# Sending each pair's spectra a second time with real and imaginary halves exchanged, so that a cross product is one full-width instruction

## The chip, the cores and the metric

The kernel runs on one core of one Trainium2 chip. The metric is the device time of one execution in microseconds; the median of three runs is given. The engines are TensorE (PE; PEld is its weight load), VectorE (DVE), ScalarE (ACT), GpSimd (POOL) and SyncE (SP, which only issues DMAs here).

## The reference, cut to what matters

The program is one block of a network: a convolution part with a filter in the frequency domain, then a mixture of experts. The change lies in the filter:

```python
xp = jnp.einsum('bhwc,mc->bhwm', xc, w_pw1)
xp = star_scale * jnp.square(jax.nn.relu(xp)) + star_bias
xf = jnp.fft.rfft2(xp, axes=(1, 2), norm='ortho')
weight = jnp.einsum('bfc,hwf->bhwc', routeing.astype(cw.dtype), cw)
spatial_weight = jnp.einsum('bfc,hwf->bhwc', spatial_routeing, spatial_weights)
xs = jnp.fft.irfft2(xf * weight, s=(H, W), axes=(1, 2), norm='ortho')
out = xp * spatial_weight + xs
out = jnp.einsum('bhwm,dm->bhwd', out, w_pw2)
...
x = x + conv(ln_c(x))
t = to_tokens(x)
t = t + ffn(ln_t(t), gate_w, w1, w3, w2)      # top 2 of 8 experts
```

The batch is 16 images of 16 x 16 pixels with 128 channels (256 inside the filter). `xf * weight` is a complex product.

## The kernel before

**Stages.** The images are handled in eight pairs. Phase A (to about 100 us) computes, for each pair, the star activation, its forward transform by matmul (`forward`, copied to `spec` by `spectrum_copy`) and the two routing networks. Then the routing weights are computed and written into the table `RS` by eight DMAs of 64 KB, four partitions each (`routing_rows`: five on SP's queue, three on GpSimd's). Phase B (131 to 224 us) is the filter, with the changed code. Behind it come the routing of tokens to experts, the expert loop over 71 tiles and the weighted sum of the results.

**The spectra.** A transform of 256 pixels is split by the parity of the vertical frequency into two parts, e = 0 and 1, of 128 rows each. In `spec[:, e, pair, :]` partition n holds a real component and partition n + 64 the imaginary component of the same frequency; the 512 columns are two images times 256 channels.

**The complex product** takes two products and a sum. TensorE writes the filter's weights for a pair into three PSUM banks in turn (`filters`, six matmuls a pair, waited for by `b_w`). VectorE's `filter_products(i, e)` forms `prod` (spectrum times real weights, L1069) and `cross` (spectrum of the *other* 64 partitions times imaginary weights). Since the two halves have to be exchanged, and a VectorE instruction has all its partitions in one order, `cross` is made by two instructions of 64 partitions, L1072 and L1073. GpSimd adds the two (`spectral`, L490), TensorE transforms back (`branch`, L817 and L823) and projects (`project`, L833).

**Order in phase B.** Every engine runs through its own fixed list; semaphores tie them together. VectorE's list for step i (`phase_b`) is: `filter_products(i + 1, 0)`, `residual(i - 1)` with the statistics of the tokens (L1078, L954, L958), `filter_products(i + 1, 1)`, `normalise_tokens(i - 1)` (L964, four instructions), `logit_copy(i - 2)` (L1090). GpSimd's is: `spatial(i + 1)` (two products, L484), `inv_std(i - 1)` (L427, L429), `spectral(i + 1)` (two sums, L490). SP's list there is only `store_tn`: for each pair one DMA of 256 KB that writes the normalised tokens `xn` to `tn_dram`, after waiting for `b_norm`. Steps 0 to 2 and 7 are written out, 3 to 6 are a hardware loop of two steps a turn. SP's list is cut differently: steps 0, 1, 6 and 7 are written out.

**Names.** `b_cross` counts finished cross products, two a pair; `a_spec` counts finished spectrum copies; `b_norm` normalised pairs; `r_mm` is set when the matmuls that read `rw2` (a table of the routing network) are done.

Of the kernel before, what the change touches and what calls it, by code (L numbers as in the profile page):

```python
# [18 lines left out]
ALU = mybir.AluOpType  # L19
# [7 lines left out]
ds = bass.ds  # L27

P = 128
# [147 lines left out]
def metaformer(nc, io):  # L177
    with ExitStack() as ctx:
# [65 lines left out]
        shared = sb("shared", [P, 7680])  # L244
        rw2 = sb("rw2", [P, NF * MED])
        idx_g = [sb(f"idx_g{u}", [P, 4], U32) for u in range(2)]
        idx_s = [sb(f"idx_s{u}", [P, 4], U32) for u in range(2)]
# [17 lines left out]
        def area(tensor, first_col):  # L265
# [63 lines left out]
            "r_log r_max r_sub r_exp r_sum r_rec r_norm r_tr r_hi r_lo r_rows r_rows_pool b_w b_sw b_p b_cross b_u b_y "  # L329
            "b_vt b_vts b_w2 b_t b_stats b_aggr b_eps b_rstd b_norm b_tn0 b_tn1 b_tr b_tnt "  # L330
            "b_gate b_logit q_iota q_zero q_tri q_dve q_ready q_exp_done q_count q_oh_tile q_oh_ready q_oh_used "
# [28 lines left out]
        def _(sp):  # L360
# [30 lines left out]
            routing_rows(sp, range(5), "r_rows")  # L391

            def store_tn(i, u):
                sp.wait_ge(S["b_norm"], i + 1)
                sp.dma_start(tn_dram[ds(i * (4 * P), 4 * P), :].rearrange("(p q) d -> p q d", p=P),
                             xn[:, u, :, :]).then_inc(S[f"b_tn{u}"], 16)
            pair_loop(sp, store_tn)

# [552 lines left out]
        def _(dve):  # L951
# [111 lines left out]

            def filter_products(i, e):

# [5 lines left out]
                dve.wait_ge(S["b_w"], i * 6 + n_s + 1)  # L1071
                dve.tensor_tensor(cross[e][0:64], spec_at(64, P, e, i), ps_w[n_s % 3][0:64, :], ALU.mult)  # L1072
                dve.tensor_tensor(cross[e][64:P], spec_at(0, 64, e, i), ps_w[n_s % 3][64:P, :], ALU.mult)\  # L1073
                    .then_inc(S["b_cross"], 1)
# [52 lines left out]
            def phase_b(i, u):  # L1127
                if not last(i, PAIRS):
                    filter_products(i + 1, 0)
                if not first(i):  # L1130
                    residual(i - 1, 1 - u)
                if not last(i, PAIRS):
                    filter_products(i + 1, 1)
                else:

                    dve.wait_ge(S["q_iota"], 8 + BUFS)
                    dve.wait_ge(S["b_logit"], PAIRS - 3)
                    top_two(0, EARLY)
                if not first(i):
                    normalise_tokens(i - 1, 1 - u)  # L1140
                if not isinstance(i, int) or 2 <= i < PAIRS - 1:
                    logit_copy(i - 2, u)
            filter_products(0, 0)
            filter_products(0, 1)
            spectrum_copy(PAIRS - 1)
# [189 lines left out]
```

## Time and profile before

| | |
|---|---|
| median of 3 runs | 529.23 us (526.0 to 530.99) |
| span of the profiled execution, first to last instruction | 477.8 us |
| median less that span | 51.4 us |
| mean granted TensorE clock over the span | 0.893 |
| filter phase, one pair (VectorE, 183.18 to 194.20 us) | 11.02 us |
| of it busy: TensorE, VectorE, GpSimd, ScalarE | 9.62, 10.63, 6.21, 2.90 us |
| VectorE busy over the span | 272.9 us, 57% |

### The profile page before, as it was taken

The page shows a single profiled execution, that of the slowest core. Times are in us where ns is not written, and L with a number is a line of the kernel's source. Part 1 is how long each engine was busy: PE and PEld are TensorE (multiplying, and loading weights), DVE is VectorE, ACT ScalarE, POOL GpSimd, SP SyncE. Part 2 cuts the span into 40 slices and gives each one's busy share as a digit, 9 for nine tenths or more (in the row PEclk, how much of TensorE's full clock was granted, in tenths as well). Part 3 has the DMA queues.
Part 4 walks back from the last instruction along what each step waited for, and adds up shares of the span by engine and source line. Part 5 has one row for each costly group of instructions (what it writes and reads, how often), then busy time and mean ns, then how long its engine had stood idle before and what let it go on. Part 6 is the DMA issues. An engine that isn't in the chain of part 4 may idle for free.

```text
span 477.8 us, 8130 instructions
## 1 busy us (share of the span) xinstructions
PE 359.2 (75%) x2236; PEld 292.9 (61%) x2237; DVE 272.9 (57%) x673; ACT 162.8 (34%) x374; POOL 260.3 (54%) x267
## 2 busy tenths in 40 slices
PE   0899999895199988875007699999999999998500
PEld 0555555393058777764006599887987888887400
DVE  5367675614077999996898554444434444433245
ACT  0454543302013223211400355443444444443253
POOL 7333342512176655541650667777777777777444
PEclk9999999978579999999555599999999999998955
DMA  8920000000200000004600111111111111112194
GB/s 249 248 63 1 2 0 0 1 5 9 35 1 1 23 22 32 34 24 152 287 0 1 45 40 54 50 52 49 54 51 49 55 50 49 52 54 50 42 358 162
DMA packets 14081, 29.94 MB, mean 63 GB/s; under 512 B 4392, under 2 KB 5564, under 8 KB 13548
## 3 DMA queue, kind: packets, MB, share of 16 engines
q1 hardware_dynamic: 7388, 17.93, 12.1%
q0 software_dynamic: 4784, 9.52, 6.7%
q10 hardware_dynamic: 1888, 2.23, 1.3%
q8 instruction: 11, 0.18, 0.2%
q14 instruction: 10, 0.08, 0.1%
HBM read 20.24 MB, written 8.85 MB: 61 GB/s over the span
## 4 chain that ended last, share of the span: by engine, by line
PE 35%; DVE 26%; DMA 13%; issue 12%; POOL 8%; ACT 2%; DVEq 1%; POOLq 1%; SPq 1%; ACTq 0%
PE bank L927 8%; DVE xn L964 7%; DMA y_dram<-shared,idx_s 7%; PE bank L909 6%; PE bank L902 3%; DMA RS<-r_hl 3%; PE bank L772 2%; PE bank L715 2%; PE bank L723 2%; POOL shared L490 2%; DVE st L954 2%; DMA shared<-tn_dram,idx_g 2%; PE bank L734 2%; DVE spec L1179 2%; PE bank L888 2%
## 5 line engine op out<-in xcount | busy, mean ns | idle before, releaser
L518 POOL DMA_INDIRECT shared<-tn_dram,idx_g x71 | 68.8, 968 | 39.9 <-DVE idx_g L1217 18.6
L527 POOL DMA_INDIRECT y_dram<-shared,idx_s x71 | 70.0, 986 | 27.1 <-issue 12.8
L909 PE MATMUL bank<-spec,shared 128*128 x426 | 61.2, 280 | 1.8 <-DVE shared L1233 0.7
L1247 DVE TENSOR_TENSOR shared<-shared,bank 128x384 f32<-128x384 f32 x71 | 39.3, 554 | 36.4 <-ACT shared L672 35.4
L672 ACT ACTIVATE shared<-bank 128x384 f32<-128x384 f32 x71 | 34.8, 490 | 64.3 <-PE bank L927 64.3
L909 PEld LDWEIGHTS bank<-spec,shared 128*128 128x128 f32 x426 | 53.5, 193 | 5.1 <-issue 5.0
L927 PE MATMUL bank<-RS,xgt_hl 128*128 x142 | 55.5, 391 | 0.6
L964 DVE TENSOR_SCALAR xn<-T,mv,rstd 128x128 f32<-128x128 f32 (+1 forms) x64 | 51.4, 874 | 5.1 <-POOL rstd L429 4.6
L927 PE MATMUL bank<-w_hi,xgt_hl 128*128 x142 | 48.9, 345 | 0.0
L427 POOL TENSOR_SCALAR var_eps<-mv 128x4 f32<-128x4 f32 x16 | 3.7, 229 | 68.7 <-DVE mv L958 68.6
L1228 DVE TENSOR_TENSOR xgt_hl<-bank,xgt_hl 128x128 fp32r<-128x128 f32 x71 | 20.6, 290 | 33.7 <-ACT xgt_hl L660 33.7
L902 PE MATMUL bank<-ident,shared 128*128 128x128 f32 x213 | 36.0, 278 | 4.5 <-DVE shared L1247 4.5
L660 ACT ACTIVATE xgt_hl<-bank 128x128 fp32r<-128x128 f32 x71 | 19.7, 277 | 57.8 <-PE bank L896 57.8
L799 PE MATMUL bank<-RS,coef 128*128 128x512 f32 (+1 forms) x48 | 21.4, 503 | 22.3 <-DMA RS<-r_hl 15.7
L927 PE MATMUL bank<-w_lo,xgt_hl 128*128 x142 | 37.3, 345 | 0.0
L665 ACT ACTIVATE shared<-bank 128x384 f32<-128x384 f32 x71 | 34.5, 486 | 5.9 <-PE bank L902 5.8
L734 PE MATMUL bank<-xp,sp 128*64 128x256 f32 x288 | 33.8, 388 | 0.0
L902 PEld LDWEIGHTS bank<-ident,shared 128*128 128x128 f32 x213 | 27.0, 142 | 10.8 <-DVE shared L1247 8.7
L823 PE MATMUL bank<-inv,shared 128*128 128x256 f32 x128 | 30.4, 380 | 1.8 <-POOL shared L490 1.8
L927 PEld LDWEIGHTS bank<-RS,xgt_hl 128*128 128x128 f32 x142 | 27.5, 194 | 5.7 <-issue 5.2
L734 PEld LDWEIGHTS bank<-xp,sp 128*64 128x64 f32 x288 | 20.2, 139 | 13.3 <-issue 4.2
L927 PEld LDWEIGHTS bank<-w_hi,xgt_hl 128*128 128x128 f32 x142 | 27.7, 195 | 0.0
(171 smaller groups left out, 680.0 us busy)
## 6 DMA issues: line engine op xcount, KB each, us to landing
star<-y_dram SPq DMA_DIRECT2D x16, 256.0 KB, 5.4
star<-in_w SPq DMA_DIRECT2D x2, 1536.0 KB, 8.5
tn_dram<-xn SPq DMA_DIRECT2D x8, 256.0 KB, 2.0
out<-T ACTq DMA_DIRECT2D x8, 256.0 KB, 2.3
spec<-in_w SPq DMA_DIRECT2D x1, 1536.0 KB, 13.2
shared<-in_sp_even SPq DMA_DIRECT2D x1, 1280.0 KB, 13.2
shared<-tn_dram,idx_g POOLq DMA_INDIRECT x71, 2.5
y_dram<-shared,idx_s POOLq DMA_INDIRECT x71, 2.2
```

Source lines behind the costliest of these rows:

```text
L518: pool.indirect_dma_start(xg[b], None, tn_dram, bass.IndirectOffsetOnAxis(ap=idx_g[quad][:, col:col + 1], axis=0)).then_inc(S[f"g_x{b}"], 16)
L527: pool.indirect_dma_start(y_dram, bass.IndirectOffsetOnAxis(ap=idx_s[quad][:, col:col + 1], axis=0), yo[b], None).then_inc(S[f"y_out{b}"], 16)
L665: act.activation(hidt[u], p_ht[u][:, 0:HID], ACT.Copy).then_inc(S["f_hts"], 1)
L672: act.activation(silu[u], p_h1[u][:, 0:HID], ACT.Silu).then_inc(S["f_silu"], 1)
L734: mm = pe.matmul(ps_conv[u][HALF * g:HALF * g + HALF, 0:PIX], sp1[:, t, :], xp[:, u, g, t // 3:t // 3 + SIZE, t % 3:t % 3 + SIZE], start=( ...
L799: pe.matmul(ps_w[n % 3][:, :], coef[:, ring[n], :], RS[:, :, :, ds(i, 1), :].rearrange("r c g b m -> r g c (b m)"), start=True, stop=True)\
L823: mm = pe.matmul(ps_v[u][m][:, g * PIX:(g + 1) * PIX], y_c[u][e][:, g * MED + m * P:g * MED + (m + 1) * P], inv[:, e, :], start=False, sto ...
L902: mm = pe.transpose(p_ht[u][:, c * P:(c + 1) * P], hid[u][:, c * P:(c + 1) * P], ident[:, :])
L909: mm = pe.matmul(p_y[:, 0:DIM], hidt[u][:, c * P:(c + 1) * P], w2s[:, c, ds(e * DIM, DIM)], start=(c == 0), stop=(c == HC - 1))
L927: mm = pe.matmul(psum[:, 0:HID], xgt[u][xs], w_hl[ws][:, cols], start=(n == 0), stop=(n == 2))
L964: op = dve.tensor_scalar(xn[:, u, t, :], flat(T[:, ds(i * 4 + t, 1), :]), mv[:, u, t, 0:1], rstd[:, u, t:t + 1], ALU.subtract, ALU.mult)
L1247: dve.tensor_tensor(hid[u], silu[u], p_h3[u][:, 0:HID], ALU.mult).then_inc(S["f_act"], 1)
```

## The change

SP sends each pair's spectra once more, from `spec` into one of two buffers of 128 partitions x 1024 columns, with partitions 0 to 63 and 64 to 127 exchanged. That is two DMAs a pair, of 64 partitions x 2 parts x 2 KB, 256 KB each. The buffers are used in turn: `rw2`, free once the routing matmuls are done, for even pairs, and the new `turned_b` for odd ones. Pairs 0 and 1 are sent behind SP's routing rows. Pair i + 2 is sent in SP's step i, ahead of that step's store of normalised tokens, after waiting for the spectrum copy and for the cross products of pair i. VectorE's cross product of both halves is then one instruction, which waits for the pair's two DMAs (`b_turned0`, `b_turned1`, 32 counts a pair).

```diff
+        turned_b = sb("turned_b", [P, NF * MED])
+        turned = [t[:].rearrange("p (e n) -> p e n", e=2) for t in (rw2, turned_b)]
...
+            def turn_spectrum(i, u):
+                wait_apart(sp, S["a_spec"], i * 2 + 2)
+                wait_done(sp, S["b_cross"], i * 2 - 2)
+                for lo, hi in ((0, 64), (64, 0)):
+                    sp.dma_start(turned[u][lo:lo + 64], spec[hi:hi + 64, :, ds(i, 1), :].rearrange("p e i n -> p e (i n)"))\
+                        .then_inc(S[f"b_turned{u}"], 16)
+
             def store_tn(i, u):
                 sp.wait_ge(S["b_norm"], i + 1)
                 sp.dma_start(tn_dram[ds(i * (4 * P), 4 * P), :].rearrange("(p q) d -> p q d", p=P),
                              xn[:, u, :, :]).then_inc(S[f"b_tn{u}"], 16)
-            pair_loop(sp, store_tn)
+            sp.wait_ge(S["r_mm"], 1)
+            turn_spectrum(0, 0)
+            turn_spectrum(1, 1)
+
+            def turn_and_store(i, u):
+                if not deferred(i):
+                    turn_spectrum(i + 2, u)
+                store_tn(i, u)
+            pair_loop(sp, turn_and_store)
...
-            def filter_products(i, e):
+            def filter_products(i, u, e):
...
                 dve.wait_ge(S["b_w"], i * 6 + n_s + 1)
-                dve.tensor_tensor(cross[e][0:64], spec_at(64, P, e, i), ps_w[n_s % 3][0:64, :], ALU.mult)
-                dve.tensor_tensor(cross[e][64:P], spec_at(0, 64, e, i), ps_w[n_s % 3][64:P, :], ALU.mult)\
+                dve.wait_ge(S[f"b_turned{u}"], (i - u) * 16 + 32)
+                dve.tensor_tensor(cross[e], turned[u][:, e, :], ps_w[n_s % 3][:, :], ALU.mult)\
                     .then_inc(S["b_cross"], 1)
```

`deferred(i)` is true for steps 6 and 7, which have no pair i + 2. The calls of `filter_products` pass the buffer's number.

SP's list before, from the routing rows into the loop (the two `tn_dram` DMAs ahead of the loop are the stores of pairs 0 and 1):

```order
L352 DMA RS<-r_hl 4x32x128 [waits rs_zero,r_lo,r_hi]
L352 DMA RS<-r_hl 4x32x128 x4
L395 DMA tn_dram<-xn 128x512 [waits b_norm] x2
L132 UNCONDITIONAL_BRANCH
L132 ISA
L395 ISA [waits b_norm]
L395 DMA tn_dram<-xn 128x512
```

and in the changed kernel at the same place:

```order
L401 DMA rw2<-spec 64x2x512 [waits a_spec,r_mm]
L401 DMA rw2<-spec 64x2x512
L401 DMA turned_b<-spec 64x2x512 [waits a_spec]
L401 DMA turned_b<-spec 64x2x512
L401 DMA rw2<-spec 64x2x512 [waits b_cross,a_spec]
L401 DMA rw2<-spec 64x2x512
L406 DMA tn_dram<-xn 128x512 [waits b_norm]
L401 DMA turned_b<-spec 64x2x512 [waits b_cross,a_spec]
L401 DMA turned_b<-spec 64x2x512
L406 DMA tn_dram<-xn 128x512 [waits b_norm]
```

The transfers of pair 3, the last ones here into `turned_b`, stand behind the store of pair 0; in the same way those of pairs 4 to 7 stand behind the stores of pairs 1 to 4.

VectorE's list before, in step 1 (products of pair 2, residual of pair 0):

```order
L1069 TENSOR_TENSOR shared<-spec,bank 128x512 [waits b_y,b_w]
L1072 TENSOR_TENSOR shared<-spec,bank 64x512 [waits b_w]
L1073 TENSOR_TENSOR shared<-spec,bank 64x512
L1078 TENSOR_TENSOR T<-T,bank 128x512 [waits b_w2]
L954 BN_STATS st<-T 128x6 [waits b_t]
```

and in the changed kernel at the same place:

```order
L1088 TENSOR_TENSOR shared<-spec,bank 128x512 [waits b_y,b_w]
L1092 TENSOR_TENSOR shared<-rw,bank 128x512 [waits b_turned0,b_w]
L1097 TENSOR_TENSOR T<-T,bank 128x512 [waits b_w2]
L973 BN_STATS st<-T 128x6 [waits b_t]
```

One instruction stands where two stood, with one more wait ahead of it. (`rw` in a name is `rw2`; `shared` holds `prod` and `cross`, `bank` is PSUM.)

## Rows read from the trace of the kernel before

**Rows 1.** The page's first part: busy time, share of the span, instructions.

```profile
PE 359.2 (75%) x2236; PEld 292.9 (61%) x2237; DVE 272.9 (57%) x673; ACT 162.8 (34%) x374; POOL 260.3 (54%) x267
```

**Rows 2.** VectorE's timeline, one pair: start, duration, engine, line, operation, idle before.

```profile
178.92 0.68 DVE L1069 TENSOR_TENSOR shared<-spec,bank 128x512 f32<-128x512 f32 x1
179.62 0.68 DVE L1072 TENSOR_TENSOR shared<-spec,bank 64x512 f32<-64x512 f32 x1
180.32 0.69 DVE L1073 TENSOR_TENSOR shared<-spec,bank 64x512 f32<-64x512 f32 x1
...
185.32 4.48 DVE L964 TENSOR_SCALAR xn<-T,mv,rstd 128x128 f32 x4
...
189.94 0.68 DVE L1069 TENSOR_TENSOR shared<-spec,bank 128x512 f32<-128x512 f32 x1
```

**Rows 3.** Busy time by stretch (the columns are named in the first line).

```profile
core 0: us, PE busy (x) PEld busy (x) DVE busy (x) ACT busy (x) POOL busy (x), PEclk, DMA share, GB/s
183.18:194.20 11.02, 9.62 (x60) 8.16 (x58) 10.63 (x21) 2.90 (x5) 6.21 (x6) 1.00 0.06 24
94.00:96.00 2.00, 0.00 (x0) 0.00 (x0) 1.94 (x4) 0.84 (x2) 2.00 (x4) 0.86 0.00 0
8.00:14.00 6.00, 1.09 (x4) 0.72 (x4) 3.84 (x9) 1.22 (x1) 5.45 (x5) 1.00 1.14 397
14.00:22.00 8.00, 7.19 (x32) 4.68 (x34) 2.17 (x4) 3.38 (x7) 1.09 (x1) 1.00 1.01 209
...
179.80:180.60 0.80, 0.80 (x6) 0.78 (x7) 0.79 (x2) 0.59 (x2) 0.00 (x0) 1.00 0.84 328
...
118.00:130.00 12.00, 0.00 (x0) 0.00 (x0) 0.00 (x0) 0.00 (x0) 3.08 (x3) 0.50 0.34 39
```

**Rows 4.** Timeline: GpSimd's last product and the last normalise instruction of a pair; a later normalise.

```profile
177.42 1.27 POOL L484 TENSOR_TENSOR shared<-star,shared 128x512 f32<-128x512 f32 x1
...
177.47 1.31 DVE L964 TENSOR_SCALAR xn<-T,mv,rstd 128x128 f32 x1
...
215.82 1.12 DVE L964 TENSOR_SCALAR xn<-T,mv,rstd 128x128 f32<-128x128 f32 x4
```

**Rows 5.** GpSimd's timeline for the pair of rows 2.

```profile
183.35 0.23 POOL L427 TENSOR_SCALAR var_eps<-mv 128x4 f32<-128x4 f32 x1 [4.65 <-DVE mv L958]
183.73 1.04 POOL L429 TENSOR_TENSOR rstd<-var_eps,mhalf 128x4 f32<-128x4 f32 x1 [0.15 <-POOL var_eps L427]
184.74 2.50 POOL L490 TENSOR_TENSOR shared<-shared 128x512 f32<-128x512 f32 x2
187.19 2.53 POOL L484 TENSOR_TENSOR shared<-star,shared 128x512 f32<-128x512 f32 x2
```

**Rows 6.** The chain that ended last, start of the filter phase: start, us, what.

```profile
115.63 0.61 SPq L352
...
118.07 12.03 DMA RS<-r_hl
...
132.57 0.68 DVE shared L1072
...
147.91 0.69 DVE shared L1073
148.63 0.70 DVE T L1078
```

**Rows 7.** TensorE's timeline: the forward transform of pair 7.

```profile
133.18 3.48 PE L723 MATMUL bank<-buf,fwd 128*128 128x512 f32 x4
```

**Rows 8.** SP's timeline: issue of a load to 64 partitions; issue of a store of tokens.

```profile
9.56 0.59 SPq L377 DMA_DIRECT2D shared<-in_sp_even  x1
...
178.96 0.35 SPq L395 DMA_DIRECT2D tn_dram<-xn  x1
```

**Rows 9.** DMA issues by line: KB each, median us from issue to landing.

```profile
tn_dram<-xn SPq DMA_DIRECT2D x8, 256.0 KB, 2.0
```

More of the change, by code:

```diff
@@ L329, in metaformer @@
             "r_log r_max r_sub r_exp r_sum r_rec r_norm r_tr r_hi r_lo r_rows r_rows_pool b_w b_sw b_p b_cross b_u b_y "
-            "b_vt b_vts b_w2 b_t b_stats b_aggr b_eps b_rstd b_norm b_tn0 b_tn1 b_tr b_tnt "
+            "b_vt b_vts b_w2 b_t b_stats b_aggr b_eps b_rstd b_norm b_turned0 b_turned1 b_tn0 b_tn1 b_tr b_tnt "
             "b_gate b_logit q_iota q_zero q_tri q_dve q_ready q_exp_done q_count q_oh_tile q_oh_ready q_oh_used "
@@ L1128, in phase_b @@
                 if not last(i, PAIRS):
-                    filter_products(i + 1, 0)
+                    filter_products(i + 1, 1 - u, 0)
                 if not first(i):
@@ L1132, in phase_b @@
                 if not last(i, PAIRS):
-                    filter_products(i + 1, 1)
+                    filter_products(i + 1, 1 - u, 1)
                 else:
@@ L1142, in phase_b @@
                     logit_copy(i - 2, u)
-            filter_products(0, 0)
-            filter_products(0, 1)
+            filter_products(0, 0, 0)
+            filter_products(0, 0, 1)
             spectrum_copy(PAIRS - 1)
```

## Prediction

> **What bounds the kernel now.** I started at the page's totals [rows 1]: no engine is full over the span, so shares say nothing and the stage of the change has to be read by itself. That stage is the filter phase, from about 131 to 224 us. VectorE's timeline for one pair [rows 2] shows no gaps: the reader should lay the starts end to end and find the first product of the next pair 11.02 us after this one (178.92 to 189.94). The table by stretch [rows 3] has the same 11.02 us with 10.63 us of VectorE, 9.62 of TensorE and 6.21 of GpSimd. TensorE has 1.4 us of slack and its clock is at its upper level of 2.4 GHz (granted 1.00).
>
> VectorE is not bound by its own work alone. The normalise takes 4.48 us in this stretch [rows 2] and 1.12 us when GpSimd is quiet [rows 4]. GpSimd's timeline [rows 5] says why: once the aggregate is done it computes var_eps and rstd, then two sums (L490) and two products (L484), 184.74 to 189.72. Each of the four normalise instructions ends just behind one of these four: the last product starts at 177.42 and ends at 178.69, the last normalise starts at 177.47 and ends at 178.78 [rows 4]. So the loop that sets the 11.02 us is: cross product of spectrum part 0, residual, statistics, aggregate (VectorE), then rstd and four full-width operations (GpSimd), whose end frees the last normalise, then the product and again the cross product. The cross product of part 1 runs beside GpSimd's rstd and is not in the loop.
>
> **What is removed.** Sixteen products lose one of their two half instructions. The second half starts 0.70 us after the first [rows 2], and the full-width product of the same 512 columns takes 0.68 us, as much as one half; so each saves 0.70 us of VectorE, 11.2 in all. What of it lies on the path:
> - Part 0 of pairs 2 to 7 is in the loop (for pair 2 the chain runs through L1073 at 147.91 straight into the residual at 148.63 [rows 6]): 6 x 0.70 = 4.2 us.
> - Part 1 of these pairs: nothing. The normalise would begin at 184.8 instead of 185.32, since rstd ends at 184.77 [rows 5], but GpSimd's first sum has started at 184.74 and the last of the four still ends at 189.72.
> - Pair 0: nothing. Behind its products come the copies of pair 7's spectrum, and these need the forward transform that TensorE has in work from 133.18 to 136.66 [rows 7]. Pair 1: its products lie beside TensorE, for which VectorE waits again before pair 2.
>
> How the normalise gives way decides the term for part 1. The trace: 1.12 us becomes 4.48, in four steps that end with GpSimd's four instructions. The Trainium skill (SBUF — State Buffer, "Who interferes with whom") says that VectorE and GpSimd share a port pair under "an exclusive lock" and that the loser waits out the whole instruction. By that rule an earlier start buys nothing, as I have it; if the two only shared bandwidth, a start 0.5 us earlier would give some 0.5 us more per pair, 3 us in all. The rows side with the rule.
>
> **What is added.** Per pair two transfers of 256 KB from SBUF to SBUF, 64 partitions each, on SP's queue, and a wait of the cross product on both. What matters is where SP issues them. For pairs 3 to 7 they stand directly behind a store of normalised tokens: SP takes up the transfers of pair i+3 only after it has issued the store of pair i, and that waits for the normalise of pair i. In VectorE's order this normalise is the last long piece before the products of pair i+3: in the trace its end (178.78) lies 0.84 us before the cross product (179.62). So whatever the transfers need beyond 0.84 us stops VectorE, five times, and queued behind the stopped cross product are the residual, the statistics, the aggregate, and through it GpSimd's rstd and the next normalise. The buffer's release (the cross products of pair i+1 done) came long before and isn't what SP waits for.
>
> Time from the end of the normalise: the store is issued 0.18 us later (178.96) and keeps SP for 0.35 [rows 8], so to 0.53; with 0.1 for registers (my estimate, from the 0.18 before) the first transfer is issued at 0.65. A transfer over 64 partitions keeps SP for 0.59 (the table load at 9.56 [rows 8]), so the second is issued at 1.25. The store's bytes move from 179.8 to 180.6, 0.84 after its issue [rows 3], and it has landed 2.0 us after its issue [rows 9]: 0.36 for the last leg. So the engines are busy with the store from 1.02 to 1.82, and the first transfer's bytes could start at 1.49 but follow at 1.82. The rate: loads over 128 partitions moved 397 GB/s, and then, when the tables of 64 partitions were in flight, 209 [rows 3]. These transfers are of the second kind: 262,144 bytes / 209 GB/s = 1.25 us each. End of bytes 1.82 + 2 x 1.25 = 4.32, landed 4.68. The stop is 4.68 - 0.84 = 3.84 us.
> - Lower end: both move at 397 GB/s, 0.66 each: landed at 3.50, stop 2.66.
> - Upper end: reading and writing 64 partitions each cost 1.25 and don't overlap: landed at 7.2, stop 6.3. The only SBUF to SBUF rows of size, the routing rows, do worse (five of 64 KB in 14.5 us, from the issue at 115.63 to 130.10, where the landing lets TensorE go [rows 6]), but each goes to 4 partitions; I leave them as a warning, not as a rate.
> I take 3.84, from the row of the same shape. Five stops: 19.2 us (13.3 to 31.7).
>
> The Trainium skill (SBUF — State Buffer, "The DMA setup-cost knee") gives a transfer 2 us plus its bytes at 436 GB/s. For the 256 KB store that is 2.6 us, where the row has 2.0. For both new transfers as one of 512 KB, issued at 0.65, it would be 3.2 us, landed at 3.85, a stop of 3.0 and five of them 15.0: 4.2 us less than my term. The row's own duration is used.
>
> **The start of the phase.** SP issues the transfers of pairs 0 and 1, 1 MB, right behind the routing rows, whose landing TensorE awaits (12.03 us of the chain [rows 6]). Queued later they can't go first, but they load the same engines and partitions. Bounds: 0, and 5.0 us (1 MB at 209 GB/s) if the routing rows had to wait for all of it. I take 1.0, near the low end, since they move only 39 GB/s from 118 to 130 [rows 3]. Pair 0's own transfers cost nothing: its cross product came at 132.57 [rows 6], 2.5 us after the routing rows; without that cover it would be up to 2.5 more. Pair 2's are issued once pair 0's products are done, near 136, and have until 147. One wait I cost at nothing: the store of normalised tokens now shares its queue, but its buffer is needed two pairs, 22 us, later.
>
> **TensorE's clock.** A stop of VectorE leaves TensorE idle, about 1.4 + 3.1 us in a pair. From 94 to 96 us it did nothing, and the granted clock fell from 1.00 to 0.50 (mean 0.86 [rows 3]), its level of 1.2 GHz. It may fall here too, but a pair then has 14.2 us for 9.62 us of matmuls, so a few microseconds at half speed fit in. I take 0, at most 2 in the tail behind pair 7.
>
> **Sum.** 19.2 - 4.2 + 1.0 = +16.0 us. The span of the profiled execution is 477.8 us; the median of the runs shown is 529.2, 51.4 more, which lies around the span and isn't touched. 529.2 + 16.0 = 545.2 us, 3.0% slower.
>
> **Rivals.**
> - *The transfers overlap or run at full rate* (stop 2.66): 13.3 - 4.2 + 1.0 = +10.1, 539.3 us. For it: one goes to the upper and one to the lower 64 partitions. Against: tables for both halves were in flight together from 14 to 22 us and moved 209 GB/s.
> - *Reading and writing in series* (stop 6.3): +28.5, 557.7 us. Against it: no row shows a transfer that pays twice.
> - *The transfers are hidden and only the saving counts.* The place is VectorE's cross product of part 0; the price is nothing and the gain 4.2, less 1.0 at the start: 526.0 us, a little faster, not measurably. It decides once the transfers land within 0.84 us of the normalise's end; at a stop of 0.6 us per pair the two sides balance. Against it: the shortest landing of 256 KB is 2.0 us, and SP has to issue the store first.
> - *TensorE becomes the bound*: if the clock stays at 1.2 GHz the 9.62 us become 19.2 against 14.2, five times 5.1 more: 570.6 us. Against it: after each stop comes dense work.
>
> **How the numbers follow.** Forecast 0.55, full rate 0.22, in series 0.10, hidden 0.06, clock 0.05, and 0.02 for something slower that I don't see. Range 536 to 556: it takes in the full rate with no cost at the start, and a stop near 5.5; outside are the hidden case, the clock and most of the series case. A measurement can tell about 1% (5.3 us) from no change. Faster by more 0.02, within 0.06, slower 0.92.
>
> **What would show it.** In the changed trace: cross products of 0.69 us, 16 in all; an idle of 3 to 4 us ahead of that of part 0 for pairs 3 to 7 alone, released by the transfer, and none for pairs 0 to 2; a pair's period near 14.2; the normalise still at 4.4; the two transfers issued within 1.3 us of the store. It is wrong if SP reaches the transfers before the store (no idle), if the idle ends with TensorE, or if the routing rows land several microseconds later.

## The result and the profile after

The changed kernel takes 553.88 us (median of 4 runs, 553.36 to 554.66); the kernel before, timed beside it, 529.45 us (4 runs, 526.0 to 530.99). The ratio is 1.0475, with a 95% interval of 1.0435 to 1.0515: 24.4 us slower, where 16.0 were forecast. Ratios leave out executions that lie over 1.5% above the fastest of their kernel; the traced execution of one experiment, the one without transfers, is of that kind, so only lengths inside its filter phase are read from it.

The page of the changed kernel, first part, against [rows 1]: VectorE has 16 instructions and 9.8 us less to do, and the kernel is slower all the same.

```profile
PE 378.2 (68%) x2236; PEld 313.3 (57%) x2237; DVE 263.1 (48%) x657; ACT 161.5 (29%) x374; POOL 260.9 (47%) x267
```

VectorE's timeline, changed kernel, from pair 3's cross product of part 0 to pair 4's (start, duration, line, operation, in brackets the idle time before and what ended it):

```profile
165.36 0.69 DVE L1092 TENSOR_TENSOR shared<-turned_b,bank 128x512 f32<-128x512 f32 x1 [5.21 <-DMA turned_b<-spec]
165.97 0.68 DVE L1097 TENSOR_TENSOR T<-T,bank 128x512 f32<-128x512 f32 x1
...
169.45 4.98 DVE L983 TENSOR_SCALAR xn<-T,mv,rstd 128x128 f32<-128x128 f32 x4 [0.30 <-POOL rstd L448]
174.35 0.18 DVE L1109 COPY logits<-bank 128x32 f32<-128x32 f32 x1
174.45 0.67 DVE L1088 TENSOR_TENSOR shared<-spec,bank 128x512 f32<-128x512 f32 x1
179.62 0.69 DVE L1092 TENSOR_TENSOR shared<-rw,bank 128x512 f32<-128x512 f32 x1 [4.50 <-DMA rw<-spec]
180.23 0.68 DVE L1097 TENSOR_TENSOR T<-T,bank 128x512 f32 x1
```

Against [rows 2] the reader should see two things. The cross product is one instruction of 0.69 us (L1092), and the residual (L1097) starts 0.61 us behind it. And the cross product of part 0 waits for the transfer: 5.21, 4.50, 4.63, 4.86 and 5.01 us for pairs 3 to 7, together 24.2, and not at all for pairs 0 to 2. The residuals of the next pairs follow at 194.90, 209.81 and 224.86, so a pair takes 14.3 to 15.1 us instead of 10.7 to 11.0.

SP's timeline of the changed kernel: L356 are the routing rows, L401 the new transfers, L406 the store of normalised tokens.

```profile
115.34 2.98 SPq L356 DMA_DIRECT2D RS<-r_hl  x5
118.42 1.83 SPq L401 DMA_DIRECT2D rw<-spec  x2
120.29 4.16 SPq L401 DMA_DIRECT2D turned_b<-spec  x2
138.03 1.27 SPq L401 DMA_DIRECT2D rw<-spec  x2
159.58 0.35 SPq L406 DMA_DIRECT2D tn_dram<-xn  x1
160.04 1.28 SPq L401 DMA_DIRECT2D turned_b<-spec  x2
174.45 0.34 SPq L406 DMA_DIRECT2D tn_dram<-xn  x1
175.32 1.36 SPq L401 DMA_DIRECT2D rw<-spec  x2
```

From 159.58 on each pair of transfers stands directly behind a store that waits for the normalise, as the prediction read from the order. Pair 4 by its own terms: the normalise ends at 174.43, the first transfer is issued at 175.32. The table by stretch shows its bytes (last column GB/s; the first row is the store's):

```profile
175.30:176.00 0.70, 0.70 (x5) 0.57 (x4) 0.00 (x0) 0.00 (x0) 0.00 (x0) 1.00 0.92 363
176.40:176.80 0.40, 0.40 (x5) 0.33 (x4) 0.00 (x0) 0.40 (x2) 0.00 (x0) 1.00 0.55 133
176.80:177.20 0.40, 0.40 (x5) 0.40 (x4) 0.00 (x0) 0.40 (x1) 0.00 (x0) 1.00 0.87 189
177.20:177.60 0.40, 0.40 (x4) 0.35 (x3) 0.00 (x0) 0.04 (x1) 0.00 (x0) 1.00 1.03 200
177.60:178.00 0.40, 0.40 (x4) 0.35 (x3) 0.00 (x0) 0.00 (x0) 0.00 (x0) 1.00 0.87 195
178.00:178.40 0.40, 0.40 (x4) 0.35 (x3) 0.00 (x0) 0.00 (x0) 0.00 (x0) 1.00 1.03 369
178.40:178.80 0.40, 0.40 (x4) 0.35 (x3) 0.00 (x0) 0.00 (x0) 0.00 (x0) 1.00 0.70 225
178.80:179.20 0.40, 0.40 (x5) 0.40 (x4) 0.00 (x0) 0.23 (x1) 0.00 (x0) 1.00 0.00 0
176.60:178.70 2.10, 2.10 (x13) 1.92 (x12) 0.00 (x0) 0.64 (x2) 0.00 (x0) 1.00 0.95 248
```

The last row takes nearly all the bytes of the pair together: they flow from 176.6 to 178.7, at 189 to 200 GB/s up to about 178.0 and faster, up to 369, in the last 0.7 us. On average that is 248 GB/s, somewhat more than the 209 of [rows 3]. The cross product starts at 179.62, 0.9 us behind the last of them.

At the start of the phase, the chain that ended last and TensorE's timeline, against the 12.03 us of [rows 6]:

```profile
117.78 15.92 DMA RS<-r_hl
```

```profile
133.79 3.19 PE L818 MATMUL bank<-RS,coef 128*128 128x512 f32 x6 [19.55 <-DMA RS<-r_hl]
...
231.09 3.48 PE L842 MATMUL bank<-inv,shared 128*128 128x256 f32 x8 [2.94 <-POOL shared L509]
```

The routing rows land 3.6 us later than before (TensorE started at 130.19 there). While they are under way, the DMA engines are busy for 0.96 of the time, where [rows 3] had 0.34 (changed kernel):

```profile
118.00:130.00 12.00, 0.00 (x0) 0.00 (x0) 0.00 (x0) 0.00 (x0) 2.81 (x3) 0.53 0.96 98
```

The last row of TensorE's timeline is eight inverse transforms behind pair 7, for the most part at half the clock; before, the same eight took 1.99 us:

```profile
209.31 1.99 PE L823 MATMUL bank<-inv,shared 128*128 128x256 f32 x8 [1.78 <-POOL shared L490]
```

The granted clock over the phase was 0.86, where before it was 1.00 (changed kernel first, then the kernel before; each row from the residual of pair 0 to that of pair 5):

```profile
151.00:224.86 73.86, 59.95 (x312) 51.55 (x310) 46.98 (x91) 15.48 (x27) 31.20 (x31) 0.86 0.19 54
```

```profile
148.63:203.10 54.47, 48.87 (x295) 41.49 (x294) 52.79 (x100) 14.87 (x26) 31.04 (x30) 1.00 0.06 24
```

**The sum by the trace.** Start +3.60; stops +24.2; products faster -6.0 (1.17 up to pair 0's residual, then 0.96 to 0.98 in each of the five intervals between residuals, stop taken off, as the one with pair 4's stop: 14.26 - 4.50 = 9.76 against 10.73); tail behind the residual of the step that forms pair 7's products +1.09 (22.37 against 21.28 us to the first reduction of the last routing step, at 247.23 and 224.36). Together +22.9 at that point; the measured 24.4 has an interval of 23.0 to 27.3 us.

One statement of the prediction about the time around the span was wrong, and the profiled execution of the kernel before wasn't one near the median of its runs. The profiled run of the changed kernel took 554.66 us in all with a span of 552.9: hardly 2 us lie around it. The 51.4 us between the span before and the median of its runs lie inside the span, in the expert loop behind the filter phase. The same stretch of 180 us of that loop, kernel before and changed kernel:

```profile
270.00:450.00 180.00, 171.67 (x1130) 154.45 (x1128) 76.52 (x244) 82.50 (x211) 132.90 (x136) 0.98 0.17 50
```

```profile
270.00:450.00 180.00, 135.47 (x828) 123.57 (x828) 68.29 (x202) 56.52 (x145) 96.03 (x98) 0.86 0.12 36
```

TensorE does 1130 matmuls in it before and 828 after: in the second trace it stands still for some 2 to 3 us about every 10 us, and the other engines do little meanwhile (from 354 to 355 us ScalarE is busy for 0.12 us, the other engines not at all). Whether this was a second effect of the change had to be asked first.

### The profile page after: what moved, and what is told of

Read it like the earlier page. It is cut to its first block, busy times and chain, and to the rows that moved or that the text cites. A ratio compares the mean times of both kernels' runs of the same rounds, so it can differ in the third digit from the quotient of the medians.

```text
span 552.9 us, 8159 instructions
## 1 busy us (share of the span) xinstructions
PE 378.2 (68%) x2236; PEld 313.3 (57%) x2237; DVE 263.1 (48%) x657; ACT 161.5 (29%) x374; POOL 260.9 (47%) x267
## 3 DMA queue, kind: packets, MB, share of 16 engines
q1 hardware_dynamic: 9692, 22.13, 14.3%
## 4 chain that ended last, share of the span: by engine, by line
PE 39%; DVE 20%; issue 14%; DMA 8%; another core or an unknown queue 6%; ACT 5%; POOL 4%; SPq 2%; DVEq 1%; POOLq 0%; ACTq 0%
PE bank L946 10%; PE bank L928 8%; DVE xn L983 7%; PE bank L921 3%; DMA RS<-r_hl 3%; PE bank L742 2%; DMA turned_b<-spec 2%; PE bank L791 2%; PE bank L915 2%; PE bank L734 2%; POOL shared L509 2%; PE bank L842 2%; DVE st L973 2%; PE bank L818 2%
## 5 line engine op out<-in xcount | busy, mean ns | idle before, releaser
L928 PE MATMUL bank<-spec,shared 128*128 x426 | 68.7, 302 | 41.8 <-ACT shared L684 27.1
L928 PEld LDWEIGHTS bank<-spec,shared 128*128 128x128 f32 x426 | 59.0, 209 | 49.5 <-issue 49.2
L946 PE MATMUL bank<-RS,xgt_hl 128*128 x142 | 58.2, 410 | 0.3
L983 DVE TENSOR_SCALAR xn<-T,mv,rstd 128x128 f32<-128x128 f32 (+1 forms) x64 | 54.1, 917 | 6.9 <-POOL rstd L448 6.6
L946 PE MATMUL bank<-w_hi,xgt_hl 128*128 x142 | 51.0, 359 | 0.0
L446 POOL TENSOR_SCALAR var_eps<-mv 128x4 f32<-128x4 f32 x16 | 3.7, 230 | 88.2 <-DVE mv L977 88.1
L921 PE MATMUL bank<-ident,shared 128*128 128x128 f32 x213 | 38.6, 294 | 8.3 <-issue 4.5
L921 PEld LDWEIGHTS bank<-ident,shared 128*128 128x128 f32 x213 | 29.1, 151 | 14.4 <-issue 7.5
L818 PEld LDWEIGHTS bank<-RS,coef 128*128 128x128 f32 x48 | 10.3, 230 | 39.7 <-issue 24.5
L946 PEld LDWEIGHTS bank<-RS,xgt_hl 128*128 128x128 f32 x142 | 29.7, 209 | 1.5 <-issue 1.3
L946 PEld LDWEIGHTS bank<-w_hi,xgt_hl 128*128 128x128 f32 x142 | 29.8, 210 | 0.0
```

The source lines that it names most:

```text
L818: pe.matmul(ps_w[n % 3][:, :], coef[:, ring[n], :], RS[:, :, :, ds(i, 1), :].rearrange("r c g b m -> r g c (b m)"), start=True, stop=True)\
L921: mm = pe.transpose(p_ht[u][:, c * P:(c + 1) * P], hid[u][:, c * P:(c + 1) * P], ident[:, :])
L928: mm = pe.matmul(p_y[:, 0:DIM], hidt[u][:, c * P:(c + 1) * P], w2s[:, c, ds(e * DIM, DIM)], start=(c == 0), stop=(c == HC - 1))
L946: mm = pe.matmul(psum[:, 0:HID], xgt[u][xs], w_hl[ws][:, cols], start=(n == 0), stop=(n == 2))
L983: op = dve.tensor_scalar(xn[:, u, t, :], flat(T[:, ds(i * 4 + t, 1), :]), mv[:, u, t, 0:1], rstd[:, u, t:t + 1], ALU.subtract, ALU.mult)
```

## Experiments

Three groups, each on one chip with runs of the kernel before beside it: the first two saw 476.5 and 475.9 us for the kernel before, the third 533.8. So differences and ratios are compared, and one length from the traces: from TensorE's first filter matmul (the landing of the routing rows) to the first reduction of the last routing step. It is 94.2 us before and 113.4 after, in the two traces above.

### Does the change cost anything outside its stage?

**The kernel before, once more, and the change, once more** (no edit).

> The kernel before, unchanged, to see what its traces are like: the profiled execution shown first had a span of 477.8 us, while the changed kernel's span lies only 1.8 us below its own time. Theory A: that execution was of a rarer, faster kind, and the 51.4 us between it and the median lie inside the expert loop, which ran from about 267 to 449 us there; then this trace has a span near 527 us and a loop of about 230 us, with the filter phase unchanged (first product near 131.9, a pair in 11.02 us). Theory B: the 51 us lie outside the span; then the span is near 478 again. Time 529 in either case.

> The changed kernel, unchanged, beside the kernel before on one chip. In the last comparison the kernel before took 476.5 us, not 529. If the change costs only what its own stage shows, the difference stays: 22.9 us from the traces' filter phase, 499.5 us where before takes 476.5, ratio 1.048. Rival (the change also slows the expert loop, where its trace showed pauses and that of before none): the difference would be 75 us, as between the two spans (552.9 and 477.8), ratio 1.157.

Measured: the kernel before took 476.86 us beside 476.51 of the same kernel (ratio 1.0005, 0.9983 to 1.0028), with a span of 473.4 and a loop without pauses: 1125 matmuls from 270 to 450 us. Both theories of the first expectation name 529 us, and neither could be decided here, since this chip doesn't show that time. The third group decides: there the kernel before took 533.8 us with a span of 532.1, so the missing 51 us lie inside the span, as theory A had it. In the trace of a kernel of the same time there (the straight halves below) TensorE does 861 matmuls in the 180 us. The time goes with the chip, not with the kernel. The changed kernel took 500.08 us beside 475.88 (ratio 1.052, 1.0473 to 1.0567): +24.2 us where the loop doesn't pause, +24.4 where it does. Its stops were 4.49, 4.51, 4.63, 4.86 and 5.40 us, its routing rows landed after 15.95 us. So the pauses go with the chip, and the change costs only its own stage.

### Is it the place of the transfers in SP's queue?

**Transfers sent two steps earlier.** SP's loop is written out, and the transfers of pair i+4 stand ahead of the store of pair i:

```diff
+            turn_spectrum(2, 0)
+            turn_spectrum(3, 1)
+            for i in range(PAIRS):
+                if i + 4 < PAIRS:
+                    turn_spectrum(i + 4, i % 2)
+                store_tn(i, i % 2)
```

> SP's list is written out, and each pair's transfers stand two steps earlier: pairs 0 to 3 ahead of the first store, pair i + 4 ahead of the store of pair i, each still waiting for the cross products that free its buffer. My theory (the stop is SP's order: the transfers queue behind the wait for the normalise): all five stops of 4.5 to 5.2 us go, a pair takes 11.02 - 0.80 = 10.2 us, and with the late start (3.6 us) the time is about 529.5 - 4.8 + 3 = 528 us, ratio 0.997. Rival (the traffic itself is what costs, through the engines or the partitions it shares): a wait stays ahead of most cross products and the time stays above 540 us.

Measured: 473.98 us beside 476.51 (ratio 0.9949, 0.9924 to 0.9973). SP now issues pair 5's transfers at 162.39, ahead of the store at 167.65, and no cross product waits for a transfer in the phase. That SP's list is written out here isn't what removes the stops: the changed kernel's step 1, which sends pair 3, is written out too and has a stop of 5.21 us. VectorE's timeline of this kernel, one pair:

```profile
167.65 0.67 DVE L1088 TENSOR_TENSOR shared<-spec,bank 128x512 f32<-128x512 f32 x1
168.24 0.67 DVE L1092 TENSOR_TENSOR shared<-rw,bank 128x512 f32<-128x512 f32 x1
168.84 0.67 DVE L1097 TENSOR_TENSOR T<-T,bank 128x512 f32 x1
...
177.60 0.67 DVE L1088 TENSOR_TENSOR shared<-spec,bank 128x512 f32<-128x512 f32 x1
```

A pair takes 9.95 us, 1.07 less than before, where my expectation had 10.2. The same work with the same bytes stands 2.5 us (1.3 to 3.6) below the kernel before instead of 24 above it: the stops come from the place in the queue. The start stays late (15.71 us for the routing rows).

**And the first transfers ahead of the routing rows.** To the edit above is added:

```diff
-            routing_rows(sp, range(5), "r_rows")
...
+            turn_spectrum(1, 1)
             sp.wait_ge(S["r_mm"], 1)
             turn_spectrum(0, 0)
-            turn_spectrum(1, 1)
+            routing_rows(sp, range(5), "r_rows")
```

> As the run before, and the transfers of pairs 0 and 1 are issued ahead of the five routing rows instead of behind them. If the routing rows land late because 1 MB shares their engines: TensorE's first filter matmul comes at 130.2 us again instead of 133.8, and the time is 529.5 - 4.8 = 524.7 us, ratio 0.991. Rival (the late landing has another cause, as the rows' own rate): no gain over the run before.

Measured: 469.35 us beside 476.51 (ratio 0.986, 0.9823 to 0.9897). It beats the kernel before by 7.2 us and the change by some 31. SP issues pair 1's transfers at 102.76 and pair 0's at 109.04, and the routing rows behind them at 114.58 take 11.28 us, as long as in kernels without any transfer (11.3 to 12.7 us over five traces).

**The change with only this second edit** (SP's order in the phase as in the change).

> The change with one edit: the transfers of pairs 0 and 1 are issued ahead of the routing rows instead of behind them; the later ones stay where they were. If the late start and the five stops add up: TensorE's first filter matmul comes 3.6 us earlier than with the change and the stops are unchanged, before + 24.4 - 3.6 = before + 20.8 us, ratio 1.044. Rival (the stops hide part of the late start): the gain over the change is under 1.5 us.

Measured: 494.78 us beside 475.88 (ratio 1.0402, 1.0366 to 1.0438), 5.3 us less than the change where 3.6 had been expected. The routing rows took 11.59 us and the five stops stayed (4.32 to 5.14). The two traces of this group say where the rest comes from: TensorE starts 4.06 us earlier than in the repeated change (129.78 against 133.84), and from there to the first residual pass 16.07 us instead of 17.28, because the forward transform of pair 7 takes 1.93 us with the clock at its upper level (granted 1.00) where it took 3.2 at the lower (0.50). That 1.2 us is luck of the moment at which the clock rose, not an effect of the edit.

### Do transfers beside VectorE's work cost anything, and where does the saving come from?

**The transfers alone.** They are sent in the change's places; VectorE keeps its two half instructions and waits for no transfer before the end of the phase. SP's list is written out, and SP waits for a buffer's last transfers before it sends the next (not shown in the cut).

```diff
-                dve.wait_ge(S[f"b_turned{u}"], (i - u) * 16 + 32)
-                dve.tensor_tensor(cross[e], turned[u][:, e, :], ps_w[n_s % 3][:, :], ALU.mult)\
+                dve.tensor_tensor(cross[e][0:64], spec_at(64, P, e, i), ps_w[n_s % 3][0:64, :], ALU.mult)
+                dve.tensor_tensor(cross[e][64:P], spec_at(0, 64, e, i), ps_w[n_s % 3][64:P, :], ALU.mult)\
```

> The transfers as in the change, but VectorE makes each cross product by the two half-width instructions of before and doesn't wait for them, save once behind the last; SP waits for a buffer's last transfers before it sends the next, and its list is written out. If only the wait costs: a pair in 11.02 us and only the late start stays, before + 3.6 us, ratio 1.008. Rival (transfers slow the engines that work beside them): a pair takes visibly longer than 11.02 us, before + 10 us or more.

Measured: 481.7 us beside 475.88 (ratio 1.0142, 1.0099 to 1.0186), +5.8. Routing rows 16.09 us; then residuals 11.01 us apart (172.41, 183.42, 194.43, 205.44), as before, and 94.17 us from landing to the last routing step, the length before to the hundredth. So 3 MB of transfers beside VectorE, GpSimd and TensorE cost these nothing. The start gives 3.5 us of the 5.8. The remaining 2.3 (1.2 at the interval's low end) lie behind the phase, 0.9 of it in the profiled run, and were not settled.

**The saving alone.** The kernel before without transfers, with one full-width cross product for both parts, of the spectrum as it lies:

```diff
-                dve.tensor_tensor(cross[e][0:64], spec_at(64, P, e, i), ps_w[n_s % 3][0:64, :], ALU.mult)
-                dve.tensor_tensor(cross[e][64:P], spec_at(0, 64, e, i), ps_w[n_s % 3][64:P, :], ALU.mult)\
+                dve.tensor_tensor(cross[e], spec_at(0, P, e, i), ps_w[n_s % 3][:, :], ALU.mult)\
```

> The kernel before without any transfer, but with the cross product of both spectrum parts as one full-width instruction that reads the spectrum as it lies (real and imaginary partitions are not exchanged, so its output is not the filter's; everything else is the same). It isolates what the change saves. Before takes 476 on this chip. Theory A (from the runs so far: a pair that took 11.02 us takes 9.94 where no stop is left): six or seven pairs save 1.08 us each, 468.5 to 469.5, with the first product of the filter phase where it was, near 130.7, and starts 0.60 us apart instead of 0.70. Rival B (the prediction's own count: six half instructions of 0.70 us on the path): 471.8. Rival C (part of the gain of the reordered kernels came from their transfers or their other order): 473 or more.

Measured: 528.21 us beside 533.81 (ratio 0.9875, 0.9824 to 0.9926), some 6.7 us less, 4.0 to 9.4 by the interval. The time alone doesn't exclude rival B's 4.2 us. The trace does: a pair takes 9.95 us, and the phase's length is 88.1 us, 6.1 less than before. Theory A holds: this is what the full width is worth, and the best version keeps it all (87.4 us).

**Part 1 alone at full width** (the edit above for `e == 1` only; part 0 keeps its two halves).

> As the run without transfers, but only the cross product of spectrum part 1 is one full-width instruction on the spectrum as it lies; part 0 keeps its two half instructions. Theory A (the normalise behind part 1 ends with GpSimd's last instruction whenever it begins, so part 1 saves nothing): within 1 us of before, 475 to 476.5, with the normalise as much longer as it begins earlier. Rival B (VectorE and GpSimd share bandwidth, so an earlier start is an earlier end): some 0.5 us a pair, 472.5 to 473.5.

Measured: 531.35 us beside 533.81 (ratio 0.9956, 0.9921 to 0.9991), so 0.5 to 4.2 us less, an interval in which both theories find room; the pair in the trace decides. The pair, in VectorE's timeline of this kernel:

```profile
192.38 0.69 DVE L1069 TENSOR_TENSOR shared<-spec,bank 128x512 f32<-128x512 f32 x1
192.99 0.68 DVE L1073 TENSOR_TENSOR shared<-spec,bank 128x512 f32<-128x512 f32 x1
194.09 4.90 DVE L964 TENSOR_SCALAR xn<-T,mv,rstd 128x128 f32 x4 [0.42 <-POOL rstd L429]
198.91 0.18 DVE L1094 COPY logits<-bank 128x32 f32 x1
```

The normalise now waits for rstd (0.42 us) and takes 4.90 us instead of 4.48; GpSimd's last product runs from 196.40 to 198.91 and sets its end. The residuals come 10.89 us apart, 0.13 less than before: of some 0.9 us that VectorE saves at part 1, 0.13 reaches the next pair. It lies behind GpSimd's last product: the next product starts 0.10 us after its end (199.01 against 198.91), where the kernel before took 0.22 (189.94 [rows 2] against 189.72 [rows 5]). Rival B's 0.5 us a pair falls. But "saves nothing" isn't right either: 0.9 us are won up to pair 0's residual, where I had counted nothing, and 1.7 us in the phase.

**Straight halves.** Two half instructions as before, each reading the 64 partitions that it writes:

```diff
-                dve.tensor_tensor(cross[e][0:64], spec_at(64, P, e, i), ps_w[n_s % 3][0:64, :], ALU.mult)
-                dve.tensor_tensor(cross[e][64:P], spec_at(0, 64, e, i), ps_w[n_s % 3][64:P, :], ALU.mult)\
+                dve.tensor_tensor(cross[e][0:64], spec_at(0, 64, e, i), ps_w[n_s % 3][0:64, :], ALU.mult)
+                dve.tensor_tensor(cross[e][64:P], spec_at(64, P, e, i), ps_w[n_s % 3][64:P, :], ALU.mult)\
```

> The kernel before with its two half instructions left, but each reads the spectrum at the same 64 partitions that it writes (no exchange, so its output is not the filter's). It asks where the 0.70 us from one half to the next instruction comes from, against 0.60 behind full-width ones. Theory A (it is a property of instructions on fewer partitions, exchanged or not): starts 0.70 apart as before, same time, 475 to 477. Rival B (reading at one set of partitions and writing at the other costs 0.1 us): starts 0.60 apart, 0.25 us less in a pair, near 474.

Measured: 533.90 us beside 533.81 (ratio 0.9998, 0.9964 to 1.0032). In the trace a pair takes 10.90 us, 0.12 less than before, and the phase 93.4, 0.8 less, which is inside the interval of the times (1.8 us to either side). VectorE's timeline of this kernel:

```profile
188.16 0.68 DVE L1069 TENSOR_TENSOR shared<-spec,bank 128x512 f32<-128x512 f32 x1
188.75 0.67 DVE L1072 TENSOR_TENSOR shared<-spec,bank 64x512 f32<-64x512 f32 x1
189.44 0.69 DVE L1073 TENSOR_TENSOR shared<-spec,bank 64x512 f32<-64x512 f32 x1
190.16 0.69 DVE L1078 TENSOR_TENSOR T<-T,bank 128x512 f32 x1
```

Neither theory holds as written: one step of the two is shorter, the other is not. What follows a half starts 0.69 or 0.72 us behind it, exchanged or not; the first half starts 0.59 us behind the full-width product, where the exchanged one took 0.70 [rows 2]. So in these traces an instruction begins 0.1 us before the one ahead of it ends if both are of full width, or a straight half follows a full width, and doesn't with a half ahead of it or an exchange; why, no run shows. That explains 0.93 us for part 0: 0.70 for the instruction, 0.23 for two closer starts.

### What is a stop made of?

**One straight transfer** of 512 KB over 128 partitions for each pair instead of two of 256 KB over 64 (unexchanged, so the products are not the filter's; VectorE's wait counts accordingly):

```diff
-                for lo, hi in ((0, 64), (64, 0)):
-                    sp.dma_start(turned[u][lo:lo + 64], spec[hi:hi + 64, :, ds(i, 1), :].rearrange("p e i n -> p e (i n)"))\
+                sp.dma_start(turned[u], spec[:, :, ds(i, 1), :].rearrange("p e i n -> p e (i n)"))\
```

> The change with one transfer of 512 KB over 128 partitions, partitions not exchanged, in place of the two of 64 partitions: the cross product is then formed of the wrong components. It tests the term that was built on the rate of 64-partition transfers. If they move 200 GB/s and those over 128 partitions 397: one issue of 0.65 us and 1.2 us of moving less in each stop, so stops of 2.8 to 3.4 instead of 4.5 to 5.2 us, and 9 us less than the change. Rival (the stop is fixed latency, not rate): stops shorter by the issue alone, 0.65 us each, 3 us less than the change.

Measured: 491.87 us beside 475.88 (ratio 1.0316, 1.0258 to 1.0374), 8.2 us less than the change. The same bytes in its table by stretch:

```profile
173.80:174.60 0.80, 0.80 (x7) 0.77 (x6) 0.00 (x0) 0.63 (x2) 0.00 (x0) 1.00 1.05 410
173.60:175.00 1.40, 1.40 (x11) 1.25 (x10) 0.00 (x0) 0.83 (x2) 0.00 (x0) 1.00 0.96 375
```

The bytes of pair 4 flow at 410 GB/s at their fastest and take 1.4 us, with stops of 3.26, 3.58 and 3.31 us for pairs 4, 6 and 7. Pairs 3 and 5 still stopped 4.83 and 5.03: for pair 3 a last trickle of 18 and 15 GB/s ran from 160.6 to 162.2, whose cause I don't know. Pair 4's stop is 1.2 us shorter than with the change, and two terms make it up: the same bytes take 1.4 us instead of 2.1, and the cross product follows them by 0.5 us instead of 0.9. The wait from the issue to the first bytes is alike, 1.3 us. So two transfers over 64 partitions cost more than one over 128, but not as I had counted it (1.2 us of rate and 0.65 for SP's second issue): the rate gives 0.7, the last leg 0.5, and the second issue nothing, since the first bytes flow only at its end.

**Only part 0 sent.** Half the bytes in as many transfers; part 1 keeps its two halves on the spectrum:

```diff
-                    sp.dma_start(turned[u][lo:lo + 64], spec[hi:hi + 64, :, ds(i, 1), :].rearrange("p e i n -> p e (i n)"))\
+                    sp.dma_start(turned[u][lo:lo + 64, 0:1, :], spec[hi:hi + 64, 0:1, ds(i, 1), :].rearrange("p e i n -> p e (i n)"))\
```

> The change for spectrum part 0 alone: its transfers carry 128 KB each instead of 256 KB, and part 1 keeps the two half instructions on the spectrum (the output is the filter's). Theory A (the stop is issue, first bytes, bytes at 195 GB/s and a last leg one behind the other; part 1 saves nothing): half of the bytes leave at most 2 x 0.67 = 1.3 us of each of five stops, so 3.5 us a stop, the start is later by about 1.8 instead of 3.6 us, and the whole takes some 491.5 where the change takes 500.1. Rival B (the time of the transfers is their rows' fixed cost and not their bytes): stops of 4.5 or more, 498 or more. Rival C (part 1's saving counted too): 494.5.

Measured: 550.12 us beside 533.81 (ratio 1.031, 1.0259 to 1.0361), +16.5 us (13.8 to 19.3), where theory A had +15.5 of its base. Stops 2.69, 2.92, 3.12, 3.27 and 4.45, together 16.5 against 24.2: 1.5 us a stop for 256 KB less, that is 170 GB/s. Some of the 1.5 is SP's: its two issues take 1.13 us instead of 1.36. So the bytes make somewhat more than half of a stop (an estimate, from 1.3 us for each 256 KB of 512 and stops of 4.84); the rest is SP's hand-over and the two ends of a transfer. The routing rows took 15.07 us, only 0.9 less than with all the bytes, where theory A had halved their delay; that the whole came out so near rests partly on this miss and the shorter stops (3.3 us on average, 3.5 expected) offsetting each other; with the one straight transfer, the same 1 MB in two instead of four, they took 12.79, hardly more than the 11.3 to 12.7 of kernels without transfers. What delays them goes with the count or form of the transfers more than with their bytes.

## Why the prediction was right, and where its sizes were off

The likeliest case came out: five stops of pairs 3 to 7 behind SP's store, none for pairs 0 to 2, released by the transfer. Its range (up to 556 us) held the time. The mechanism is shown: the same transfers two steps earlier leave no stop, the transfers without the wait leave the pair at 11.01 us, and the saving without the transfers is 6 to 7 us. The sum was 8.4 us short; the four terms below make 6.9 of it, and the rest is less than the interval of the measurement. One of the prediction's own signs of being wrong did come: the routing rows landed several microseconds later. It didn't upset the whole, since the term for the start was small beside the stops. And the normalise, which was to stay at 4.4 us, took 4.9 to 5.0.

- **The stop: 3.84 forecast, 4.84 measured on average, +5.0 us in all.** For pair 4, counted from the normalise's end at 174.43: the first bytes flowed at 2.2 us where I had 1.82, since SP's hand-over took 0.89 us instead of 0.65 and the bytes came 1.3 us after the issue; they took 2.1 us instead of 2.50; and from the last bytes to the cross product passed 0.9 us, where I had taken 0.36 from the store's last leg. So the end of the bytes, 4.3 us, was as forecast by luck, one term too short and one too long, and the last leg was mis-sized: the row of another kind of destination gave too little. What covers the transfers shrank too: the cross product would have begun 0.6 us behind the normalise, not 0.84, since the change itself brings the starts closer. The other stops differ by two things that the trace shows. For pair 6 SP's hand-over took 1.23 us, and the stop is 0.36 longer. For pair 3 a last trickle of 15 to 26 GB/s ran from 163.6 to 164.8; the repeated change had none for this pair and a stop of 4.49. Pair 7 has a weaker one, up to 223.9. What makes the trickle stays open.
- **The saving: 4.2 forecast, 6.0 measured.** The steps of 0.70 us were read as the instruction's own price; they were a consequence of half-width and exchanged instructions, and two that remain became 0.60. Part 1 gives 0.13 us a pair instead of nothing, and the first pairs 1.2 instead of nothing.
- **The start: 1.0 forecast, 3.6 measured**, inside its bounds of 0 to 5.0. The low bytes per second of the routing rows (39 GB/s) were read as room for others, and that was the wrong reading. With half the bytes in as many transfers they still took 15.07 us, so it isn't bandwidth alone that they lose. Nor is it only the engines' time: from 118 to 130 us their busy share was 0.73 there and 0.77 with the one straight transfer, and these rows landed after 15.07 and 12.79 us. What it is was not settled. With the new transfers issued ahead of them instead, the start costs nothing.
- **TensorE's clock: 0 forecast, 1.1 measured**, inside the 2 allowed. In the phase it fell to its level of 1.2 GHz behind each of the first four stops, in which TensorE had stood idle (0.50 from 167 to 173 us, for one), and came back before the next. The 1.1 us are of the tail. There TensorE did nothing in the 2.94 us before 231.09, and the clock, up to then at its upper level, fell under the eight transforms (changed kernel):

```profile
218.00:231.00 13.00, 8.00 (x54) 7.07 (x53) 7.34 (x17) 1.71 (x3) 4.15 (x5) 1.00 0.21 62
232.00:234.00 2.00, 2.00 (x7) 1.55 (x6) 1.90 (x11) 0.00 (x0) 0.23 (x1) 0.50 0.34 131
```

The rival of full rate and overlap (397 GB/s, a stop of 2.66) falls by the 248 GB/s of pair 4 and by stops that were never under 4.3; reading and writing in series would have stopped VectorE 6.3 us; the hidden case needs the other place in the queue, and there it is real, 2.5 us faster and 7.2 with the start mended; TensorE never became the bound in the five intervals: its matmuls fill 59.95 of 73.86 us.

The term for the normalise rested on two reads of the trace. The row shows an end that follows GpSimd's: 4.48 us become 4.90 when it starts earlier. The Trainium skill (SBUF — State Buffer, "Who interferes with whom") has the lock for this, and the trace agrees: GpSimd's last product sets the end of the normalise in both kernels, and the 0.13 us a pair lies behind it. The Trainium skill's setup-cost rule (SBUF — State Buffer, "The DMA setup-cost knee") gives 3.2 us for 512 KB, an estimate. For one transfer over 128 partitions the trace is near it: pair 4's cross product started 3.08 us after the issue (172.34 to 175.42). For the change's two transfers over 64 partitions it is too short: 4.30 us from the first issue (175.32 to 179.62).

## What to carry to other kernels

A transfer that replaces work of an engine is free only where its issue stands early enough in the order of its queue: look at what the instruction ahead of it in that queue waits for, before its bytes are counted. Here the same 4 MB cost 24 us behind the store of tokens; ahead of it they gained 2.5 us, and 7 with the first two pairs ahead of the routing rows as well. Send what will be needed later before small, scattered pieces that someone already waits for, not behind them. And when an instruction is split, count the starts from one to the next, not its duration: here two halves took 1.42 us from start to start (179.62 to 181.04 in the kernel before), where the one full-width instruction took 0.60.

## What the runs showed of the hardware

- VectorE's full-width products on 512 columns follow each other every 0.60 us though each is shown as 0.68, where neither has to wait; with a half of 64 partitions ahead, or a half that reads across partitions, the step is 0.69 to 0.72.
- SBUF to SBUF, 512 KB: as two queued transfers over 64 partitions it took 2.1 us (189 to 200 GB/s at first, up to 369 at the end, 248 on average), as one over 128 partitions 1.4 us (375, at most 410). The page's median from issue to landing is 3.5 and 4.0 us for the transfers of 256 KB.
- Four transfers of 256 KB behind the routing rows made these take 15.7 to 16.1 us, where without any they took 11.3 to 12.7; four of 128 KB 15.1, two of 512 KB 12.8. The fourth of the 256 KB transfers kept SP for 3.1 us (in the kernel that sends two steps earlier), where an issue later in the phase takes 0.6; the fourth of 128 KB did not.
- The same kernel took 476 us in the groups on two chips and 534 in that on a third, with pauses only in the loop of indirect transfers; what the change costs, 24 us, was the same with and without them.
